# Gated delta rule, 64 sequences on one core: rotations one sequence further ahead, scores over two steps, one straight body, four unread matmuls per step

## The reference, cut to what matters

```python
# scanned over t; for every mode m, batch b, head h
S = S * exp(g_t)
kv = k_t @ S
dv = (v_t - kv) * beta_t
S = S + outer(k_t, dv)
o_t = q_t @ S
# afterwards
o = sum over m of softmax(mode_logits)[h, m] * o_t
out = x + (o * sigmoid(x @ Wg)) @ Wo      # then an 8-expert, top-2 feed-forward part
```

## Time and profile before

| | |
|---|---|
| median of three runs | 4784.49 us |
| the profiled execution: its own time, its span | 4793.02 us, 4790.8 us |
| busy share: TensorE, VectorE, ScalarE, GpSimd | 84%, 76%, 61%, 8% |
| mean granted TensorE clock | 0.873 |
| DMA mean | 66 GB/s |

### The profile page before, as it was taken

The page is one execution under the profiler, slowest core; times in us unless marked ns, Lnnn a source line. Parts: engine busy times, 40 slices in busy tenths (PEclk is TensorE's granted clock), DMA queues, the critical chain, the costliest instruction groups (busy, mean ns, idle before and its releaser), DMA issues. The chain is left out here.

```text
span 4790.8 us, 195228 instructions
## 1 busy us (share of the span) xinstructions
PE 4015.4 (84%) x85713; PEld 3307.7 (69%) x85713; DVE 3652.5 (76%) x7742; ACT 2902.2 (61%) x9736; POOL 371.3 (8%) x156
## 2 busy tenths in 40 slices
PE   5502999889988998889889988898899889987999
PEld 2201777777777777777777777777777777775666
DVE  6754888778877887788778877887788778854655
ACT  5742666666666666666666666666566666654443
POOL 1221000000000000000000000000000000000000
PEclk8755889889888998899889988998899889988999
DMA  4675222322232223222322231223122312203110
GB/s 119 167 182 133 52 51 56 83 53 52 52 87 53 52 52 87 53 52 52 87 53 52 52 87 47 57 52 87 40 59 58 82 44 58 57 10 83 36 31 7
DMA packets 283082, 314.77 MB, mean 66 GB/s; under 512 B 135768, under 2 KB 182752, under 8 KB 278112
## 3 DMA queue, kind: packets, MB, share of 16 engines
q1 hardware_dynamic: 282208, 301.99, 26.7%
HBM read 232.70 MB, written 69.21 MB: 63 GB/s over the span
## 5 line engine op out<-in xcount | busy, mean ns | idle before, releaser
L926 DVE TENSOR_TENSOR run_SC<-run_SP,run_DB 128x512 f32<-128x512 f32 x512 | 350.1, 687 | 474.6 <-PE run_SP L1057 468.3
L943 DVE TENSOR_TENSOR run_XL<-run_XL,run_EL 128x30 f32<-128x30 f32 (+14 forms) x1920 | 637.3, 332 | 66.0
L942 DVE TENSOR_TENSOR run_EL<-run_AL,run_XL 128x30 f32<-128x30 f32 (+14 forms) x1920 | 636.7, 332 | 66.0
L1053 PE MATMUL run_SP<-run_KP 64*32 64x128 f32 x8192 | 624.8, 302 | 24.5 <-DVE run_KP L901 12.7
L980 POOL TENSOR_TENSOR run_DB<-run_DB,run_below 128x2048 f32<-128x2048 f32 x64 | 297.9, 4655 | 3613.7 <-DVE run_XL L943 3487.9
L801 ACT ACTIVATE run_DB<-run_DB,run_col 128x64 f32<-128x64 f32 x2048 | 537.3, 337 | 12.0 <-POOL run_DB L980 4.2
L1053 PEld LDWEIGHTS run_SP<-run_KP 64*32 64x32 f32 x8192 | 465.6, 119 | 101.8 <-issue 50.0
L859 ACT COPY run_S<-run_KS 128x256 f32<-128x256 f32 x448 | 166.9, 373 | 556.5 <-PE run_KS L1118 556.5
L808 ACT ACTIVATE run_KD<-run_PR,run_col 128x64 f32<-128x64 f32 x2048 | 471.6, 327 | 12.9 <-PE run_PR L1073 6.8
L846 ACT ACTIVATE run_R<-run_KS,run_col 128x64 f32<-128x64 f32 x1792 | 416.0, 323 | 102.8 <-PE run_KS L1082 102.4
L1057 PE MATMUL run_SP<-run_KP 64*32 64x64 f32 x8192 | 454.5, 243 | 0.0
(11 more groups left out here) (201 smaller groups left out, 7588.8 us busy)
## 6 DMA issues: line engine op xcount, KB each, us to landing
run_DB<-G_s SPq DMA_DIRECT2D x256, 256.0 KB
run_EG<-EG_s SPq DMA_DIRECT2D x128, 512.0 KB, 8.9
run_tab<-TAB_s SPq DMA_DIRECT2D x128, 256.0 KB, 10.5
KQ_s<-proj_win SPq DMA_DIRECT2D x32, 768.0 KB, 7.8
run_win<-KQ_s SPq DMA_DIRECT2D x64, 384.0 KB, 3.1
TAB_s<-tab_tab SPq DMA_DIRECT2D x128, 128.0 KB, 2.4
run_V<-V_s SPq DMA_DIRECT2D x128, 128.0 KB, 2.6
V_s<-proj_vv SPq DMA_DIRECT2D x64, 128.0 KB, 3.1
```

The costliest lines, as they stand in the source:

```text
L942: v.link(dve.tensor_tensor(e, bcast(AL[:, r + 1:, r], 2, done), bcast(XL[:, r, 0:done], 1, rows), ALU.mult))
L943: less = dve.tensor_tensor(XL[:, r + 1:, 0:done], XL[:, r + 1:, 0:done], e, ALU.subtract)
L1053: pe.matmul(out[64 * e:64 * e + C, p].rearrange("p (z u) i -> p z (u i)", z=2), KP[f, par, p, t0:t1], KP[f, kq, p, t0:t0 + SPAN], start=Tr ...
```

## The change

- All 67 steps (-3 to 63) are one straight body with constant addresses: no loop and no barrier within it.
- In step k the engines run k, score k+1, rotate k+2 and turn k+3. `KP` gets three planes of keys and one of queries, `col` three slots, `EG` one instead of two.
- Scores 0 to 2 (exponentials 0 to 3) of a sequence are made a step earlier ("next" in the places); score 3 stands between merges, 4 to 7 in the gaps.
- VectorE's rotation goes by halves of 256 tokens instead of quarters of 128, interleaved with the takes of the sequence before it. Each sum is waited for by VectorE itself.
- GpSimd masks `DB` in two halves: the first after the rotation's last sum, the second after the elimination. `DB` is loaded in halves.
- The places are written out by name. The last key rows and turn now lie before the end of the run on TensorE.
- Four matmuls (`stay_busy`: identity by `Sdec`, 128x128 by 256 columns, into a bank that nobody reads from them) stand two before the first merge, one after each of the first two.

```diff
-        KP = sb("KP", [128, 3, PAIRS, T])
+        KP = sb("KP", [128, 4, PAIRS, T])
...
+        PE_PLACES = [["score 4"], ["merge"], ["score 5"], ["score 6"], ["score 7"], ["keys 0"], ["next 0"], ["keys 1"],
+                     ["turn 0"], ["keys 2"], ["turn 1"], ["keys 3"], ["next 1"], ["turn 2"], ["next 2"], ["turn 3"]]
+        ACT_PLACES = [["merge"], ["exp 6"], ["exp 7"], [], [], ["keys 0"], ["keys 1"], ["keys 2"],
+                      ["keys 3", "turn 0"], ["keys 4", "next 0"], ["keys 5", "turn 1"], ["keys 6", "next 1"],
+                      ["keys 7", "next 2"], ["turn 2", "next 3"], [], ["turn 3"]]
...
+                for k in STEPS:                    # VectorE
+                    a, b = k + 1, k + 2
+                    prepares, rotates = real(a), real(b)
+                    if prepares:
+                        take(a, 0)
+                        take(a, 1)
+                        take(a, 2)
+                    if rotates:
...
+                        dve.wait_ge(act_t, 4 * (b + 1))
+                        if k > 0:
+                            dve.wait_ge(pe_o, RUNS * k)
+                        products(b, False, 0)
+                    if prepares:
+                        take(a, 3)
+                    if rotates:
+                        total(b, False, 0)
+                    if prepares:
+                        decayed(a, 0)
+                        decayed(a, 1)
+                        take(a, 4)
+                        dve.wait_ge(qd_done, DECAYED * a + 3)
+                    if rotates:
+                        products(b, True, 0)
+                    if prepares:
+                        take(a, 5)
+                    if rotates:
+                        total(b, True, 0)
+                        products(b, False, 1)
+                    if prepares:
+                        take(a, 6)
+                    if rotates:
+                        total(b, False, 1)
+                    if prepares:
+                        decayed(a, 2)
+                        decayed(a, 3)
+                        take(a, 7)
+                        dve.wait_ge(qd_done, DECAYED * a + 5)
+                    if rotates:
+                        products(b, True, 1)
+                        total(b, True, 1)
+                    if prepares:
+                        to_lanes(a)
+                        for r in range(1, C - 1):
+                            eliminate(a, r)
+                        from_lanes(a)
...
+                for n in range(NSEQ):              # GpSimd
+                    pool.wait_ge(l_ga, 64 * (n + 1))
+                    if n:
+                        pool.wait_ge(rot_q, 2 * (n + 1))
+                    only_below(0)
+                    pool.wait_ge(l_gb, 64 * (n + 1))
+                    if n:
+                        pool.wait_ge(lanes_done, n)
+                    only_below(1)
...
+                def stay_busy():
+                    pe.matmul(KS[:, 0].rearrange("p a v -> p (a v)"), ident[:, :], Sdec[:, :, :].rearrange("p a v -> p (a v)"),
+                              start=True, stop=True)
...
+                for k in STEPS:                    # TensorE
+                    if real(k):
+                        stay_busy()
+                        stay_busy()
+                        merge(k, 0, 0)
+                        stay_busy()
+                        merge(k, 0, 1)
+                        stay_busy()
+                    prepare_part(k, "score 3")
+                    if real(k):
+                        merge(k, 1, 0)
+                    for c in range(SUPER):
...
-        emit(-1, 0, 1, [(False, True, True)], first=True)
-        with nc.Fori(0, H - 1) as r:
-            emit(r * B, r, 0, [(True, True, True)] * B)
-        emit(NSEQ - B, H - 1, 0, [(True, True, k < B - 2) for k in range(B - 1)] + [(True, False, False)])
```

More of the change, by code:

```diff
@@ L626, in recurrence @@
         V = sb("V", [128, 2, SUPER, DV])
-        col = sb("col", [128, 2, 3, PAIRS, SUPER])
+        col = sb("col", [128, 3, 3, PAIRS, SUPER])
         decay = sb("decay", [128, 2, PAIRS, SUPER])
-        EG = sb("EG", [128, 2, PAIRS, T])
+        EG = sb("EG", [128, PAIRS, T])
         win = sb("win", [128, NT, 2 * WIN])
@@ L647, in recurrence @@
         OB = ps("OB", [128, NT, DV])
-        (l_win, l_gr, l_eg, l_col, l_v, l_tab, pe_t, act_t, rot_k, rot_q, pe_s, d_ready, d_exp, scored,
+        (l_win, l_ga, l_gb, l_eg, l_col, l_v, l_tab, pe_t, act_t, rot_k, rot_q, pe_s, d_ready, d_exp, scored,
          dve_s, qd_done, xt_done, pe_kd, kd_done, pe_m, act_m, pe_r, act_r, pe_w, act_w, pe_f, act_f,
-         s_dec, pe_o, act_o, stored, l_const, lanes_done) = sems[:33]
+         s_dec, pe_o, act_o, stored, l_const, lanes_done) = sems[:34]
         with nc.Block() as block:
@@ L662, in _ @@
                 dve.memset(XN[:, :, :, :], 0.0).then_inc(dve_s, 1)
+                dve.memset(Sdec[:, :, :], 0.0).then_inc(dve_s, 1)
                 for e in range(2):
@@ L665, in _ @@
                     dve.tensor_copy(ZM[rows, :, :, C:], bcast(bcast(ident[rows, rows], 1, SUPER), 1, PAIRS)).then_inc(dve_s, 1)
[L666 removed]
+                dve.wait_ge(dve_s, 9)
         fresh()
[L669 to L695, removed]
[L696 to L1182 removed]
@@ L1185, in recurrence, with real @@
-        PE_PLACES = [1, 2, 1, 1, 2, 1, 1, 1, 0, 0, 1, 1, 1, 1, 1, 1]
-        ACT_PLACES = [1, 1, 1, 1, 1, 1, 0, 0, 1, 1, 1, 2, 1, 1, 2, 0]
-        emit(-1, 0, 1, [(False, True, True)], first=True)
-        with nc.Fori(0, H - 1) as r:
-            emit(r * B, r, 0, [(True, True, True)] * B)
-        emit(NSEQ - B, H - 1, 0, [(True, True, k < B - 2) for k in range(B - 1)] + [(True, False, False)])
+        RUNS, WRITES, DECAYED = SUPER, SUPER - 1, 1 + NT
+        STEPS = range(-3, NSEQ)
+        def real(n):
+            return 0 <= n < NSEQ
@@ new lines, in bank @@
+        def bank(n, c):
+            return SP[(SUPER * n + c) % 3]
+        PE_PLACES = [["score 4"], ["merge"], ["score 5"], ["score 6"], ["score 7"], ["keys 0"], ["next 0"], ["keys 1"],
[3 more added lines that the diff above has]
+                      ["keys 7", "next 2"], ["turn 2", "next 3"], [], ["turn 3"]]
@@ L1194, in experts @@
+        fresh()
 def experts(nc, sems, fresh, x, Wg, Wo, gate_w, w13, w2, c_small, ident, XN_s, O_s, out):
```

711 lines of the change are left out of this document (364 added, 347 removed).

## The result

The changed kernel takes 4478.3 us (median of 4, 4471.13 to 4485.37) against 4780.83: a ratio of 0.937 (95% interval 0.934 to 0.940), 6.3% faster. The forecast was 4475, with 4310 to 4700 as range. The total was met; the parts of the sum were met less well, and that is what the experiments are about.

A forecast was written before the change was run, and what follows sets the result against it. TensorE with its waits was taken to set the period: 47.2 + 2.6 matmuls + 5 waits + 0.2 = 55.0 us against 58.4. That gives 214 plus 112 for jumps, less 16 for filling: 310 us less, 4475 us, range 4310 to 4700.

The forecast's parts named there:

- The straight body, 112 us: At the 8 loop boundaries: removing jumps, barriers and emptying of DMA queues saves 112 us, bounds 51 and 114.
- The period, 55.0: Per step of the recurrence: TensorE's work, unread matmuls and waits sum to 55.0 us, against 58.4 before.
- The account at half clock: In TensorE's step: work at full clock, low-clock loss and waits sum to 60.7 and 55.9 us, against measured 59.9 and 56.5.
- The four unread matmuls: Around TensorE's merges: they cost 2.6 us per step and hold the clock in nearly all steps, worth up to 6 us.
- Scores: VectorE's waits for TensorE's scores: only score 5 comes late, by 1 us, making VectorE's own period 52.2 us.
- VectorE: VectorE's rotation: 12 operations of 1024 elements at 1.11 us replace 24 of 512; its step becomes about 51.2 us.
- GpSimd beside VectorE: Mask halves on GpSimd beside VectorE: 0.55 us was lost before; now value 0 to -0.3, bound above by 2.3.
- Order at the step's end: Key rows 3 and turn 3 ahead of the last write: about 5 us of TensorE waits per step remain, in other places.
- B: Rival at the merges: clock still falls briefly, 7 us low per step, period 59.1, total 4730; 0.23 together with D.
- A: Rival: clock holds, ScalarE's waits shrink and VectorE becomes the bound, period 52.2, total 4300; chance 0.14.
- C: Slower rival: clock falls for long in each step, 17 us low, period 65.5, total 5130 (4930 with 12 low); chance 0.10.
- D: Rival: rotation ahead hides nothing, clock as now, period 58.4, only the jumps gone, 4690; 0.23 together with B.

The follow-up runs named there:

- a_two: The changed kernel with only the two unread matmuls behind the first merges, without the two ahead of the first merge: 4417 us.
- a_eight: The changed kernel with eight unread matmuls instead of four: 4581 us.
- a_s5: The changed kernel with score 5 ahead of the last merge instead of behind the first span's write: 4559 us.
- best1: a_two with the places written anew for spans 2 to 7, to avoid TensorE's waits for KD and R: 4602 us.
- best2: best1 with score 5 ahead of the last merge, as in a_s5: 4385 us.
- a_notab: a_two with the first head's tables of angles kept for all heads, leaving out the 4 MB loaded per head: 4391 us.
- a_none: The changed kernel without its four unread matmuls: 4504 us.
- b_both: The kernel before as one straight body and with the four unread matmuls, its order of work unchanged: 4597 us.
- a_narrow: The changed kernel with each of its four unread matmuls replaced by twelve of 32x32 by 32 columns: 4972 us.

## Why the prediction came out right, step by step

**The bound.** Right. TensorE with its waits was said to set the period, VectorE not. a_two, a_eight and a_s5 show it: what is added to or taken from TensorE's path comes back in the period, and taking VectorE's wait for score 5 away gives nothing. Both are close, though: best1 and best2 show that 1 to 2 us less on TensorE make VectorE the later one.

**The straight body, 112 us.** The step that failed in size. Alone it brings 68 (7 of the 8 boundaries), some 78 for all 8. The term took all that stood out in each eight steps for the boundary's. Most of what is left is the loading of 4 MB of tables, which the straight body keeps: 26 us in all by a_notab, in the new order, and 2 to 9 us in each of seven steps. "No new wait replaces it" overlooked that the load itself slows the step that it is hidden in.

**The period, 55.0.** Met in the mean (55.02), and by luck: two errors cancel. Ordinary steps take 54.0, so 63 steps give 63 us more than was put down for them. What stands out above 63 ordinary steps was 114 us before and is 3466.4 - 63 x 54.0 = 64 now, so that part fell by 50 instead of 112.

**The account at half clock.** It was said to hold within 1 us. 50.7 busy and the row's 5.5 idle make 56.2, not 55.9, against 56.5; this changes nothing. It takes all work to be twice as long at the low level; the one score measured above is 1.87 times as long.

**The four unread matmuls.** The price was 2.6 us per step. By their starts it is 2.3 (1.06 + 2 x 0.63); by a_none's steps in which the clock holds (52.2) it is 1.8, and where the other 0.5 goes wasn't traced. What they bring was given too much: "what they bring is the clock". The new order alone takes the low clock from 760 to 280 us, the matmuls alone (b_both) from 760 to 340, and only both together to 70. The forecast gave the order a part in one clause, that the idle time before the merges goes, and no term of its own. From the straight body in the old order to the change it is 236 us; matmuls first 117 and order then 119, or order first 210 and matmuls then 26. The two remove much of the same low clock, so no single split is the true one. What in the new order does it is not shown by a run that changes it alone. That it takes away TensorE's waits for TM and for the last copies ahead of the merges is the likeliest: after the first step, a first merge waits over 0.9 us in 61 of 62 steps of the kernel before and in none of the change, and in best1, where the wait came back, the clock fell at the merges only in steps that had it.

**Scores.** Score 5 was given 1 us of wait; it is 2.8 in the step shown (3.1 in the mean), and all waits for scores are 4 us per step (258.5 over 63 to 64), where under 2 was named as the sign of being right. By my count score 5 was to be ready 13.2 us after TM; it ends at 1556.4, 15.1 after. The two unread matmuls ahead (1.1) and the late end of TensorE (0.5) were left out there, and make 1.6 of the 1.9. It cost nothing, as VectorE wasn't the bound.

**VectorE.** A product of 1024 elements was to start 1.11 after the last; it is 1.13. The expected idle time before the first product, for `pe_o`, isn't there (its waits have no such row): the two ends are 0.5 us apart and three takes lie between.

**GpSimd beside VectorE.** Up to 0.3 us: the negation to `XL` beside the first half of the mask takes, in the kernel after,

```profile
1515.95 1.02 DVE L903 TENSOR_SCALAR run_XL<-run_AL 128x1024 f32<-128x1024 f32 x1
```

and alone, in the kernel before, it took

```profile
1606.27 0.69 DVE L935 TENSOR_SCALAR run_XL<-run_AL 128x1024 f32<-128x1024 f32 x1
```

That is 0.33 lost, and the 0.55 of the earlier trace rows gone.

**Order at the step's end.** About 5 us of TensorE's waits were to remain. From 500 to 3939 it is busy 3176 of 3439, so idle 4.2 per step; the places are those foreseen, KD copies 2.0 and R 0.9. **Filling:** 16 us expected; the first XO moves from 476.3 to 496.2, 20.

**Rivals.** B didn't come: the low clock is about 1 us per step, not 7. Idle time is not the whole cause of a fall: in a_narrow TensorE is idle hardly more than in the change (4.9 and 4.2 us per step), and the clock is lowest, 0.86 against 0.99. Gaps do seem to count: in best1 the clock falls at the merges in 36 of the 50 steps with a wait of over 0.9 us ahead of them and in none of the 12 others. Nor do all falls lie at the merges: of 67 between 500 and 3939 us in the kernel before, 57 begin within 12 us after XO's start and ten elsewhere, each 3.5 to 4 us long, such as the one from 1852.5 to 1856.5. A, C and D didn't come either.

## What to carry to other kernels

A time that recurs with a loop's boundary need not be the boundary's: look at what else is done once per round, count how many periods stand out in a round, and leave each thing out on its own. Where the clock depends on what an engine does, taking a wait away can hand the wait to that engine and cost more than it saved (best1: TensorE's waits for KD down from 130 to 1.8 us, clock 0.91, 186 us slower than a_two), so which of two close engines is the later should be chosen, not left. Work put in to hold the clock belongs where the thin work is (here the two matmuls between the merges did as much as four), in few large matmuls rather than many small ones (clock 0.99 and 0.86), and its number is to be tried in both directions (4581 us with eight, 4478 with four, 4417 with two, 4504 with none).

## What the runs showed of the hardware

- In half-microsecond stretches from 500 to 3939 us the granted clock is 1.00 or 0.50 but where it changes; a score takes 0.99 us at 1.00 and 1.85 at 0.50 (kernel before).
- With TensorE busy alike (3171 and 3176 of 3439 us) the granted clock is 0.86 when the fillers are 32x32 by 32 columns (a_narrow) and 0.99 when they are 128x128 by 256 (the change). Without fillers it is 0.96 (a_none), so thin filler is worse than none.
- In best1 (0.91 in the mean) the clock fell at the merges in 36 of 50 steps with a wait of 0.9 to 2.2 us ahead of them, and in none of 12 with a shorter one. In a_none it fell there in 25 steps without such a wait.
- 4 MB of loads within one step make a TensorE that needs none of their data stand for its own instructions, up to 4.0 us at once between 768 and 822 us; leaving them out takes 26 us away in all. TensorE goes on 1.3 to 1.7 us after the packet of its instruction queue has ended, in all 15 such gaps of over 1 us.
- A negation of 128x1024 on VectorE takes 1.03 us in the median of 64 in the kernel after, beside a GpSimd operation (the mask's first half from 1514.06 to 1516.43 us in the step shown), and 0.69 in the kernel before, alone.
